# Two transformer layers over 416 edge groups: scores, softmax and sums in three stages, or in one chunked loop

## The chip, the cores and the metric

The kernel runs on one core of one Trainium2 chip. The metric is the time of one execution on the device in microseconds, from a few runs, lower is better. The profile is of one further execution.

## What is computed

A chain of graph layers over 3125 nodes with 128 features and 50000 edges, sorted by destination: a relational layer, a GCN with batch norm, a GATv2 layer with a feed-forward part, and at the end two transformer convolutions. Only the last two are restructured. Each computes, with H = 4 heads of C = 32:

```python
q = (x @ Wq + bq).reshape(N, H, C)
k = (x @ Wk + bk).reshape(N, H, C)
v = (x @ Wv + bv).reshape(N, H, C)
alpha = jnp.einsum('ehc,ehc->eh', q[dst], k[src]) / jnp.sqrt(jnp.float32(C))
amax = jax.ops.segment_max(alpha, dst, num_segments=N)
ealpha = jnp.exp(alpha - amax[dst])
denom = jax.ops.segment_sum(ealpha, dst, num_segments=N)
attn = ealpha / denom[dst]
out = jax.ops.segment_sum(attn[..., None] * v[src], dst, num_segments=N)
return out.reshape(N, H * C) + x @ Ws + bs
```

## The kernel before

The nodes lie in 25 windows of 125. The sorted edges are cut into 416 tiles of 128 edges ("pairs" of an edge tile and the one window that its destinations fall in); `pair_win_i` holds each pair's window, read into registers by `windows`. Four pairs are a group (G = 4), so there are 104 groups. One transformer layer is five blocks, one after the other, with all engines joined between them:

- `conv_nodes` computes q, k, v and the skip term for all nodes and stores k and v to `kv_table` in DRAM.
- `conv_scores`: GpSimd (POOL) issues four indirect gathers a group (L917) that bring the k and v rows of the edges' sources into a ring of eight groups, `got`. SyncE (SP) stores the v half to `v_rows` in DRAM. VectorE (DVE) makes a one-hot of the destinations (L927); TensorE (PE) turns it (L1801), ScalarE (ACT) copies it (L1787), and PE multiplies it with q (L1814), in fp32. Two score banks `q_b` alternate. DVE multiplies with k (L1775), reduces by head (L1778) and scales (L1780).
- `segment_softmax` takes the maximum over each destination's edges for all 416 x 4 columns at once: transposes on PE, scans and element-wise passes on DVE, then one exponential on ACT into `small`.
- `conv_sums` runs over double groups of eight pairs: SP loads the stored v rows, DVE makes the one-hots (L1064) and the messages (L1068), GpSimd splits the weights into three bf16 parts (L998 to L1004). PE adds messages (fp32, L1092) and weights (bf16, 12 columns, L1093) into all eight PSUM banks, at the address of the pair's window, and after every second pair adds a product of 512 zero columns to the last bank (L1097). Before its loop it issues 16 of these as well (L1082).
- `conv_finish` divides, adds the skip term and normalizes at the end.

The loops of PE, DVE, ACT and SP are hardware loops (`Fori`); that of GpSimd in `conv_scores` is written out. Each engine works through its own instructions in order.

## Time and profile before

| | |
|---|---|
| median of 3 runs | 4879.6 us (4878.93 to 4885.05) |
| profiled execution, its time | 4863.76 us |
| span of that execution | 4862.0 us |
| first transformer layer, first gather to last sum read | 3181.6 to 3968.7 us |
| second transformer layer, first gather | 4026.2 us |
| mean granted TensorE clock | 0.716 |

### The profile page before, as it was taken

Reading aid. Unit: us, or ns where it says so; the run is one execution under the profiler, and the core shown is the slowest. Engines: PE = TensorE matmul, PEld = TensorE weight load, DVE = VectorE, ACT = ScalarE, POOL = GpSimd, SP = SyncE. Lnnn points to the kernel's source line nnn. Section 1 sums busy time; section 2 is a strip of 40 time slices with the busy share of each in tenths; the row PEclk is TensorE's granted clock in tenths of the full one; section 3 lists DMA queues with packets and bytes.
Section 4 is the critical chain, followed back from the end, with each engine's and each line's share of the span. In section 5 each row is a group of like instructions: output and inputs, shape, how many; then the busy total and the mean of one; then the engine's idle time right before and its main releaser. Section 6 shows DMA issues by size and latency. Waiting matters only on the chain. (4 is left out here: it accounts for less than half of the span.)

```text
span 4862.0 us, 67990 instructions
## 1 busy us (share of the span) xinstructions
PE 3211.9 (66%) x15577; PEld 2186.9 (45%) x15578; DVE 2813.1 (58%) x9606; ACT 888.8 (18%) x2002; POOL 2734.6 (56%) x3193
## 2 busy tenths in 40 slices
PE   6766677743433259999996998544443984444395
PEld 3235566633333224555543444434443863444284
DVE  8997454431111586676767888744444663444476
ACT  1000111110000021111114777311110211111021
POOL 0016677327777047555535886067774746777373
PEclk9985555555555579999998999855555995555597
DMA  1111122211111104233321221045553435555342
GB/s 61 39 38 45 43 53 53 26 33 51 50 50 50 31 1 103 77 80 79 78 46 43 67 69 49 15 141 153 152 153 93 142 100 143 153 154 154 87 150 83
DMA packets 320800, 387.80 MB, mean 80 GB/s; under 512 B 45989, under 2 KB 230133, under 8 KB 320618
## 3 DMA queue, kind: packets, MB, share of 16 engines
q0 software_dynamic: 80000, 192.10, 15.7%
q1 hardware_dynamic: 240618, 193.80, 13.2%
q14 instruction: 132, 1.08, 0.1%
q8 instruction: 50, 0.82, 0.1%
HBM read 279.89 MB, written 105.84 MB: 79 GB/s over the span
## 5 line engine op out<-in xcount | busy, mean ns | idle before, releaser
L917 POOL DMA_INDIRECT got<-kv_table,pair_src x832 | 814.9, 979 | 497.5 <-issue 252.9
L559 POOL DMA_INDIRECT y_got<-y_table,y_idx x416 | 399.0, 959 | 505.3 <-SPq L511 338.2
L927 DVE TENSOR_TENSOR hot<-pair_dst,iota 128x500 bf16<-128x500 f32 (+1 forms) x424 | 289.3, 683 | 511.0 <-PE sums L990 474.0
L917 POOL DMA_INDIRECT got<-t_table,pair_src x416 | 414.8, 997 | 267.9 <-ACTq L953 141.5
L917 POOL DMA_INDIRECT got<-x_table,pair_src x420 | 398.3, 948 | 286.2 <-issue 283.3
L1801 PE MATMUL hot_b<-ident_b,hot 128*125 128x128 bf16 x840 | 144.1, 327 | 566.5 <-DVE hot L927 566.4
L1439 DVE SCALAR_TENSOR_TENSOR junk<-z,att 128x128 f32<-128x128 f32 x1664 | 381.4, 287 | 179.1 <-PE z L1497 178.1
L1775 DVE TENSOR_TENSOR prod<-q_b,got 128x512 f32<-128x512 f32 x208 | 143.8, 692 | 570.4 <-DMA got<-kv_table,pair_src 538.8
L1493 PE MATMUL z<-gat_wl,got_t 128*128 128x512 f32 x832 | 432.1, 600 | 0.0
L990 PE MATMUL sums<-got,hot 128*125 128x128 f32 x832 | 214.7, 438 | 328.2 <-DMA got<-t_table,pair_src 328.2
L1202 PE MATMUL sums<-msg,hot 128*125 128x512 f32 x832 | 405.3, 636 | 29.2 <-POOL msg L1143 29.2
L1814 PE MATMUL q_b<-acc,hot_t 125*128 x1664 | 420.1, 434 | 0.1
L1801 PEld LDWEIGHTS hot_b<-ident_b,hot 128*125 128x125 bf16 x840 | 105.2, 217 | 628.5 <-DVE hot L927 628.5
L1814 PEld LDWEIGHTS q_b<-acc,hot_t 125*128 125x128 f32 x1664 | 380.1, 333 | 0.5 <-issue 0.5
L990 PEld LDWEIGHTS sums<-got,hot 128*125 128x125 f32 x832 | 184.3, 326 | 359.1 <-issue 359.1
L1497 PE MATMUL z<-xr,hot_t 125*128 x1248 | 336.1, 377 | 0.0
L1188 DVE TENSOR_TENSOR acc<-acc,sums 125x536 f32 x416 | 295.2, 710 | 52.5 <-PE sums L1206 8.3
L1787 ACT CAST hot_t<-hot_b 125x512 f32<-125x512 bf16 x210 | 123.2, 587 | 1010.3 <-PE hot_b L1801 1010.1
L1092 PE MATMUL sums<-msg,hot 128*125 128x128 f32 x1664 | 301.4, 296 | 5.7
L1092 PEld LDWEIGHTS sums<-msg,hot 128*125 128x125 f32 x1664 | 272.0, 188 | 32.5 <-issue 20.3
L1143 POOL TENSOR_TENSOR msg<-rows,wts 128x512 f32<-128x512 f32 x208 | 247.2, 1207 | 36.3 <-DVE wts L1172 33.4
L683 DVE SCALAR_TENSOR_TENSOR hot_w<-iota,src_loc,psum 128x125 f32<-128x125 f32 x416 | 115.2, 339 | 256.9 <-PE psum L795 256.9
(410 smaller groups left out, 6314.8 us busy)
## 6 DMA issues: line engine op xcount, KB each, us to landing
v_rows<-got SPq DMA_DIRECT2D x208, 256.0 KB, 3.2
rows<-v_rows SPq DMA_DIRECT2D x104, 512.0 KB, 3.7
x_rows<-got SPq DMA_DIRECT2D x104, 256.0 KB, 2.6
rows<-x_rows SPq DMA_DIRECT2D x104, 256.0 KB, 2.6
got<-kv_table,pair_src POOLq DMA_INDIRECT x832, 2.9
y_table<-y_stage SPq DMA_DIRECT2D x25, 500.0 KB
got<-x_table,pair_src POOLq DMA_INDIRECT x420
y_got<-y_table,y_idx POOLq DMA_INDIRECT x416, 2.5
```

Source lines behind the costliest of these rows:

```text
L559: pool.indirect_dma_start(out=got[:, slot, j, :], out_offset=None, in_=y_table[:, :], in_offset=bass.IndirectOffsetOnAxis(ap=m.y_idx[:, co ...
L917: pool.indirect_dma_start(out=self.got[:, slot, j, :], out_offset=None, in_=self.table[:, :], in_offset=bass.IndirectOffsetOnAxis(ap=self. ...
L927: v.tensor_tensor(self.hot[:, b, :, :], bc_last(m.pair_dst[:, cols], Q), bc_mid(m.iota[:, 0:Q], G), ALU.is_equal).then_inc(self.hot_ready, 1)
L990: last = t.matmul(sums[0:Q, bass.ds(ws[j] * D, D)], loop.hot[:, b, j, :], loop.got[:, slot, j, :], start=False, stop=False)
L1092: t.matmul(sums[0:Q, bass.ds(ws[j] * D, D)], hot[:, b, j, :], msg[:, b, j, :], start=False, stop=False)
L1188: v.tensor_tensor(row, row, sums[j][0:Q, 0:H * D + 6 * H], ALU.add).then_inc(read, 1)
L1202: t.matmul(sums[j][0:Q, 0:H * D], hot[:, b, j, :], msg[:, b, j, :], start=True, stop=True)
L1439: last = v.scalar_tensor_tensor(junk[:, j, h, :], z[j][:, h * D:(h + 1) * D], 0.0, m.att[:, h * D:(h + 1) * D], ALU.max, ALU.mult, accum_o ...
L1493: t.matmul(z[j][:, :], got_t[:, b, j, :], m.gat_wl[:, :], start=True, stop=False)
L1497: last = t.matmul(z[j][:, :], hot_t[:, b, j, :], m.xr3[:, bass.ds(ws[j], 1), k, :].rearrange("q o d -> q (o d)"), start=False, stop=(k == 2))
L1801: last = t.transpose(hot_b[b][0:Q, j * P:(j + 1) * P], hot[:, b, j, :], m.ident_b[:, :])
L1814: last = t.matmul(q_b[b][:, j * P:(j + 1) * P], hot_t[:, b, j, :], m.acc[:, bass.ds(w, 1), 0:D].rearrange("q o d -> q (o d)"), start=True, ...
```

## The change

`conv_scores`, `segment_softmax` and `conv_sums` of the transformer layers become one block, `conv_layer`, with all loops written out. The pairs are divided into four chunks of 32, 32, 24 and 16 groups. In each chunk, each step scores one group; in the first steps of a chunk (16, 16 and 12 of them) the step also handles two groups of the chunk before (messages on DVE, `add` on PE). At the end of each chunk comes its softmax. The last chunk's 16 groups of sums follow at the end.

Other parts of it: the one-hots for the scores are no longer turned on PE. The destinations are written once as rows to DRAM (`dst_rows`), ACT's queue loads 512 of them broadcast to 125 partitions for each group, and one DVE comparison (`turn_hot`) makes the turned one-hot. Seven PSUM banks hold sums (25 x 128 columns) and weights (25 x 4 columns); the eighth, `work`, is the single bank for scores and softmax. The weights are summed in fp32 with four columns; GpSimd's split, ACT's bf16 copy and the products with zero columns inside the sums are gone. Destinations whose edges cross a chunk's end get an extra row of their own, 125 + chunk (`pair_row`), which is scaled and added back (`rejoin`) at the end; the tables for it are worked out on DVE at the end of `gcn_nodes`. The scale of the scores moves into the weights of q. `alpha` and the scan penalties are laid out by chunk, so in `sort_edges`, `segment_softmax` (still used by the GATv2 layer) and `gat_scores` some operations are cut in four, and the DVE loop of `gat_scores` becomes four loops. The gathers are as before.

```diff
-assert TILES * P >= E and FULL + W <= PAIRS and Q * W == N
+CHUNK = (128, 128, 96, 64)
+CHUNK_AT = tuple(sum(CHUNK[:c]) for c in range(len(CHUNK)))
+assert TILES * P >= E and FULL + W <= PAIRS and Q * W == N and sum(CHUNK) == PAIRS and all(n % 32 == 0 for n in CHUNK)
...
+def chunk_view(flat, c):
+    return flat[:, H * CHUNK_AT[c]:H * (CHUNK_AT[c] + CHUNK[c])].rearrange("l (h p) -> l h p", h=H)
...
+            link(v.tensor_copy(loc[:, :], loc_b[:, 0:3]))
+            link(v.tensor_scalar(m.pair_row[:, :], m.pair_dst[:, 0:PAIRS], float(Q), float(P), ALU.is_ge, ALU.mult))
+            link(v.tensor_tensor(m.pair_row[:, :], m.pair_row[:, :], m.pair_dst[:, 0:PAIRS], ALU.add))
+            for b in range(len(CHUNK) - 1):
+                at, n = CHUNK_AT[b], CHUNK[b]
+                pairs, one = slice(at, at + n), slice(b, b + 1)
+                link(v.tensor_scalar(cont[:, one], m.cont_pen[:, at + n:at + n + 1], -1.0, None, ALU.is_gt))
...
+                link(v.tensor_scalar(mark[:, 0:n], m.pair_win[:, pairs], m.pair_win[:, at + n - 1:at + n], None, ALU.is_equal))
+                link(v.scalar_tensor_tensor(mark[:, 0:n], m.pair_dst[:, pairs], loc[:, one], mark[:, 0:n], ALU.is_equal, ALU.mult))
+                link(v.scalar_tensor_tensor(m.pair_row[:, pairs], mark[:, 0:n], move[:, one], m.pair_row[:, pairs], ALU.mult, ALU.add))
...
+            nc.vector.tensor_scalar(w4[:, 0, :], w4[:, 0, :], float(C) ** -0.5, None, ALU.mult)
+            nc.vector.tensor_scalar(b4[:, 0, :], b4[:, 0, :], float(C) ** -0.5, None, ALU.mult).then_inc(scaled, 1)
+            dve.wait_ge(scaled, 1)
...
-def conv_scores(nc, m, kv_table, v_rows):
...
+def groups_of(c):
+    return range(CHUNK_AT[c] // G, (CHUNK_AT[c] + CHUNK[c]) // G)
+def sums_due(c, k):
+    if not c:
+        return ()
+    before = groups_of(c - 1)
+    return before[2 * k:2 * k + 2]
...
+def conv_layer(nc, m, kv_table, dst_rows, v_rows):
...
+        psum = bank("psum", (P, 8 * 512))
+        dens, work = W * D, psum[:, 7 * 512:8 * 512]
...
+            def load(s):
+                sp.wait_ge(aside[s % 8], 16 * (s // 8 + 1))
+                if s >= 3:
+                    sp.wait_ge(msg_ready, s - 2)
+                sp.dma_start(rows[:, s % 3, :, :], v_rows[s, :, :].rearrange("l (j d) -> l j d", j=G)).then_inc(row_back[s % 3], 16)
+            for c in range(len(CHUNK)):
+                for k, g in enumerate(groups_of(c)):
+                    sp.wait_ge(come[g % 8], 16 * G * (g // 8 + 1))
+                    sp.dma_start(v_rows[g, :, :].rearrange("l (j d) -> l j d", j=G), got[:, g % 8, :, D:2 * D]
+                                 ).then_inc(aside[g % 8], 16)
+                    if c:
+                        due = sums_due(c, k)
+                        ahead = min(due.stop + 2 if len(due) else loaded, groups_of(c - 1).stop)
+                        while loaded < ahead:
+                            load(loaded)
+                            loaded += 1
+            while loaded < groups:
+                load(loaded)
+                loaded += 1
...
+            def turn_hot(g):
+                dve.wait_ge(row_in[g % 3], 16 * (g // 3 + 1))
+                if g >= 2:
+                    dve.wait_ge(q_done, g - 1)
+                v.tensor_scalar(hot_t[:, g % 2], dst_row[:, g % 3, :].rearrange("q (w j l) -> q w j l", w=2, j=2), m.lane[0:Q, :], None,
+                                ALU.is_equal).then_inc(hot_t_ready, 1)
+            def score(c, g):
+                at = g * G - CHUNK_AT[c]
+                dve.wait_ge(q_done, g + 1)
+                dve.wait_ge(come[g % 8], 16 * G * (g // 8 + 1))
+                v.tensor_tensor(prod[:, g % 2, :, :], work.rearrange("p (j d) -> p j d", j=G), got[:, g % 8, :, 0:D], ALU.mult
+                                ).then_inc(used, 1)
+                if g + 1 < groups:
+                    turn_hot(g + 1)
+                dve.wait_ge(used, g + 1)
+                v.reduce_sum(chunk_view(m.alpha, c)[:, :, at:at + G],
+                             prod[:, g % 2, :, :].rearrange("p j (h c) -> p h j c", h=H), AX).then_inc(scored, 1)
+            def messages(s):
+                c = 0
+                while s not in groups_of(c):
+                    c += 1
+                at = s * G - CHUNK_AT[c]
+                w = wts[:, c % 2, 0:H * CHUNK[c]].rearrange("l (h p) -> l h p", h=H)[:, :, at:at + G]
+                if s >= 2:
+                    dve.wait_ge(summed, s - 1)
+                v.tensor_tensor(hot[:, s % 2],
+                                m.pair_row[:, s * G:(s + 1) * G].rearrange("l (w j) -> l w j", w=2).unsqueeze(3).broadcast_to([P, 2, 2, P]),
+                                m.iota[:, 0:P].unsqueeze(1).unsqueeze(1).broadcast_to([P, 2, 2, P]), ALU.is_equal)
+                dve.wait_ge(row_back[s % 3], 16 * (s // 3 + 1))
+                dve.wait_ge(exped, c + 1)
+                v.tensor_tensor(msg[:, s % 2, :, :].rearrange("l j (h c) -> l j h c", h=H),
+                                rows[:, s % 3, :, :].rearrange("l j (h c) -> l j h c", h=H),
+                                w.rearrange("l h j -> l j h").unsqueeze(3).broadcast_to([P, G, H, C]), ALU.mult).then_inc(msg_ready, 1)
...
+            turn_hot(0)
+            for c in range(len(CHUNK)):
+                for k, g in enumerate(groups_of(c)):
+                    score(c, g)
+                    for s in sums_due(c, k):
+                        messages(s)
+                softmax(c)
...
+            for s in groups_of(last_chunk):
+                messages(s)
+            dve.wait_ge(shares_ready, 1)
+            dve.wait_ge(closed, 1)
+            for b in range(last_chunk):
+                w, = windows(nc, m.pair_win_i, ENG.DVE, CHUNK_AT[b + 1] - 1, 1)
...
+            for g in range(groups):
+                if g >= 3:
+                    act.wait_ge(hot_t_ready, g - 2)
+                act.dma_start(dst_row[:, g % 3, :], row_bc(dst_rows[g, :], Q)).then_inc(row_in[g % 3], 16)
+                if done < last_chunk and g == groups_of(done).stop + 2:
+                    act.wait_ge(shifted, done + 1)
+                    nc.scalar.activation(wts[:, done % 2, 0:H * CHUNK[done]], carried[:, 0, 0:H * CHUNK[done]], ACT.Exp).then_inc(exped, 1)
+                    done += 1
...
+            def query(c, k, g):
+                ws = windows(nc, m.pair_win_i, ENG.PE, g * G, G)
+                pe.wait_ge(hot_t_ready, g + 1)
...
+                if g:
+                    pe.wait_ge(used, g)
+                if c and not k:
+                    pe.wait_ge(low_read, c)
                 for j in range(G):
-                    last = t.transpose(hot_b[b][0:Q, j * P:(j + 1) * P], hot[:, b, j, :], m.ident_b[:, :])
+                    last = t.matmul(work[:, j * P:(j + 1) * P], hot_t[:, g % 2, j // 2, j % 2, :],
+                                    m.acc[:, bass.ds(ws[j], 1), 0:D].rearrange("q o d -> q (o d)"), start=True, stop=True)
+                last.then_inc(q_done, 1)
+            def add(c, s):
+                ws = windows(nc, m.pair_win_i, ENG.PE, s * G, G)
+                w = wts[:, c % 2, 0:H * CHUNK[c]].rearrange("l (h p) -> l h p", h=H)
+                pe.wait_ge(msg_ready, s + 1)
+                for j in range(G):
+                    t.matmul(psum[:, bass.ds(ws[j] * D, D)], hot[:, s % 2, j // 2, j % 2, :], msg[:, s % 2, j, :], start=False, stop=False)
+                    last = t.matmul(psum[:, bass.ds(ws[j] * H + dens, H)], hot[:, s % 2, j // 2, j % 2, :],
+                                    w[:, :, s * G + j - CHUNK_AT[c]], start=False, stop=False)
+                last.then_inc(summed, 1)
...
+                t.matmul(work[:, 0:cols], m.only127[:, :], top[:, 0:cols], start=True, stop=True).then_inc(high_ready, 1)
+                pe.wait_ge(high_read, c + 1)
+                t.matmul(work[:, 0:cols], m.only0[:, :], top[:, 0:cols], start=True, stop=True).then_inc(low_ready, 1)
...
+            for k in range(7):
+                t.matmul(psum[:, k * 512:(k + 1) * 512], zeros[:, 0:P], zeros[:, :], start=True, stop=False)
+            for c in range(len(CHUNK)):
+                for k, g in enumerate(groups_of(c)):
+                    query(c, k, g)
+                    for s in sums_due(c, k):
+                        add(c - 1, s)
+                softmax(c)
+            for s in groups_of(last_chunk):
+                add(last_chunk, s)
...
-            conv_scores(nc, m, kv_table, v_rows)
-            segment_softmax(nc, m)
-            conv_sums(nc, m, v_rows)
+            conv_layer(nc, m, kv_table, dst_rows, v_rows)
```

## Rows read from the trace of the kernel before

**Rows 1.** Page: span, and granted clock in 40 slices (tenths).

```profile
span 4862.0 us, 67990 instructions
...
PEclk9985555555555579999998999855555995555597
```

**Rows 2.** Windows: scores, softmax, sums of the first layer (columns: head row).

```profile
core 0: us, PE busy (x) PEld busy (x) DVE busy (x) ACT busy (x) POOL busy (x), PEclk, DMA share, GB/s
3181.00:3722.40 541.40, 260.70 (x1252) 230.00 (x1252) 232.68 (x418) 61.60 (x105) 409.38 (x416) 0.50 0.55 151
3722.40:3775.20 52.80, 14.07 (x42) 8.87 (x42) 30.76 (x15) 4.34 (x2) 0.08 (x1) 0.60 0.01 3
3775.20:3968.70 193.50, 185.95 (x1488) 169.42 (x1488) 134.84 (x159) 53.32 (x52) 144.22 (x209) 0.99 0.45 141
```

**Rows 3.** Groups by line, first transformer layer (busy us, mean ns, idle before).

```profile
L917 POOL DMA_INDIRECT got<-kv_table,pair_src x416 | 409.4, 984 | 304.1 <-POOLq L55 177.7 <-issue 126.4
...
L1775 DVE TENSOR_TENSOR prod<-q_b,got 128x512 f32<-128x512 f32 x104 | 71.9, 691 | 288.0 <-DMA got<-kv_table,pair_src 266.9 <-PE q_b L1814 21.0
...
L1778 DVE TENSOR_REDUCE score<-prod 128x16 f32<-128x512 f32 x104 | 71.3, 686 | 3.5
...
L1068 DVE TENSOR_TENSOR msg<-rows,wts 128x1024 f32<-128x1024 f32 x52 | 66.2, 1274 | 2.2 <-DMA rows<-v_rows 2.2
L1064 DVE TENSOR_TENSOR hot<-pair_dst,iota 128x1000 f32<-128x1000 f32 x52 | 62.4, 1200 | 0.0
```

**Rows 4.** Timeline of one group of scores (start, duration in us, engine, line).

```profile
3400.30 0.94 POOL L917 DMA_INDIRECT got<-kv_table,pair_src  x1 [0.30 <-issue]
...
3401.55 1.16 POOL L917 DMA_INDIRECT got<-kv_table,pair_src  x1 [0.30 <-issue]
...
3402.42 2.02 PE L1814 MATMUL q_b<-acc,hot_t 125*128 x8
...
3404.60 0.69 DVE L1775 TENSOR_TENSOR prod<-q_b,got 128x512 f32<-128x512 f32 x1 [2.71 <-DMA got<-kv_table,pair_src]
```

**Rows 5.** Timeline of TensorE in the sums stage, two pairs.

```profile
3783.06 0.38 PE L1092 MATMUL sums<-msg,hot 128*125 128x128 f32 x2
3783.28 0.17 PE L1093 MATMUL sums<-wts,hot_b 128*125 128x12 bf16 x1
3783.30 0.46 PE L1092 MATMUL sums<-msg,hot 128*125 128x128 f32 x2
...
3783.88 0.38 PE L1092 MATMUL sums<-msg,hot 128*125 128x128 f32 x2
```

**Rows 6.** Timeline: fp32 matmuls of 8 moving columns in the attention stage.

```profile
1701.46 1.77 PE L1316 MATMUL g_lin<-w_lin,xt 128*125 128x8 f32 x15 [0.40 <-ACT xt L257]
```

**Rows 7.** Timeline of VectorE in the softmax stage.

```profile
3730.90 3.62 DVE L155 TENSOR_TENSOR_SCAN carried<-start_turned,sg_low 128x1664 f32<-128x1664 f32 x1 [8.53 <-PE sg_low L122]
...
3756.23 1.89 DVE L172 TENSOR_TENSOR ends<-carried,cont_pen 128x1660 f32<-128x1660 f32 x1
```

**Rows 8.** Windows of other stages: TensorE busy time beside the granted clock.

```profile
600.00:640.00 40.00, 29.67 (x172) 25.68 (x170) 19.66 (x103) 6.82 (x18) 30.25 (x33) 0.50 0.21 53
1756.00:1760.00 4.00, 2.45 (x4) 0.67 (x4) 3.93 (x11) 0.94 (x3) 2.36 (x2) 0.73 0.00 0
1760.00:1764.00 4.00, 3.36 (x4) 1.15 (x4) 3.97 (x10) 1.03 (x2) 2.35 (x2) 0.50 0.00 0
...
3730.00:3732.00 2.00, 0.87 (x5) 0.47 (x3) 1.10 (x1) 0.00 (x0) 0.00 (x0) 0.82 0.00 0
```

**Rows 9.** Timeline of TensorE inside the first of these windows.

```profile
642.53 0.59 PE L788 MATMUL psum<-ident_b,hot_rel 128*24 128x128 bf16 x4 [1.29 <-DVE hot_w L683]
643.05 2.07 PE L809 MATMUL psum<-y_got,hot_w 128*125 128x128 f32 x8
644.91 0.55 PE L814 MATMUL psum<-dw_hot,dl_hot 128*125 128x32 bf16 x4
645.39 0.60 PE L795 MATMUL psum<-inv_t,rel_t 24*128 x4
```

More of the change, by code:

```diff
@@ L832, in make_link, with gcn_nodes @@
     return link
-def gcn_nodes(nc, m, ins, t_table):
+def gcn_nodes(nc, m, ins, t_table, dst_rows):
     with ExitStack() as ctx:
@@ L873, in _ @@
         def _(pe):
+            for k in range(PAIRS // RB):
+                last = nc.tensor.transpose(dst_b[0:RB, k * P:(k + 1) * P], m.pair_dst[:, k * RB:(k + 1) * RB], m.ident[:, :])
+            last.then_inc(dst_turned, 1)
+            for b in range(3):
+                at = CHUNK_AT[b + 1] - 1
+                last = nc.tensor.matmul(loc_b[:, b:b + 1], m.only127[:, :], m.pair_dst[:, at:at + 1], start=True, stop=True)
+            last.then_inc(loc_ready, 1)
             pe.wait_ge(x_ready, 1)
@@ L1714, in _ @@
             pe.wait_ge(copied, TG)
+            pe.wait_ge(scaled, 1)
             pe.wait_ge(loaded, 128)
@@ new lines, in _ @@
+            go(v.tensor_copy(m.h[:, :, :].rearrange("q w d -> q (w d)"), psum[0:Q, 0:W * D]))
+            link(v.tensor_copy(m.dens[:, :, :].rearrange("q w h -> q (w h)"), psum[0:Q, dens:dens + W * H]))
+            for b in range(last_chunk):
+                w, = windows(nc, m.pair_win_i, ENG.DVE, CHUNK_AT[b + 1] - 1, 1)
+                sums, ws = m.h[:, bass.ds(w, 1), :].rearrange("q o d -> q (o d)"), m.dens[:, bass.ds(w, 1), :].rearrange("q o h -> q (o h)")
+                dve.wait_ge(rejoined, 1)
+                go(v.tensor_tensor(sums, sums, work[0:Q, b * (D + H):b * (D + H) + D], ALU.add))
+                link(v.tensor_tensor(ws, ws, work[0:Q, b * (D + H) + D:(b + 1) * (D + H)], ALU.add))
@@ L1819, in conv_finish @@
+            for k in range(7):
+                last = t.matmul(psum[:, k * 512:(k + 1) * 512], zeros[:, 0:P], zeros[:, :], start=False, stop=True)
+            last.then_inc(closed, 1)
+            pe.wait_ge(parts_ready, last_chunk)
+            for b in range(last_chunk):
+                last = t.matmul(work[0:Q, b * (D + H):(b + 1) * (D + H)], m.rejoin[:, b, :], part[:, b, :], start=True, stop=True)
+            last.then_inc(rejoined, 1)
 def conv_finish(nc, m, last_layer, out):
```

371 lines of the change are left out of this document (191 added, 180 removed).

## The prediction

> **What bounds the kernel now.** I read the page first [rows 1]: only the last third of the span, from slice 26 on, holds the restructured layers, and there the granted clock falls to 0.5 in the scores and stands near full in the sums. The windows by stage give one layer: 541.4 us of scores, 52.8 of softmax, 193.5 of sums, together 787.7 us [rows 2]; the second layer has the same shape. The stages have different bounds. In the scores GpSimd is the pace: 416 gathers at 984 ns with 0.30 us between them [rows 3, 4] make 416 x 1.28 = 534 us, and DVE waits 266.9 us for gathers at the product L1775 [rows 3]. All else there is slack: PE is busy 260.7 of 541.4 us, at clock 0.50. In the sums PE is the pace: 185.95 busy of 193.5 us, at clock 0.99 [rows 2]. So the idea of laying the sums under the gathers has up to some 193 + 53 us a layer to win. The question is whether a step with both is shorter than what it replaces, and at which clock PE does it.
>
> **What one pass costs.** Eight fp32 passes of 128 columns take 2.02 us in the scores, with 0.3 us of run-out some 0.21 us each; this is clock 0.50 [rows 4, 2]. In the sums a pair of pairs repeats every 0.82 us (3783.06 to 3783.88): four such passes, two small bf16 products and one of 512 zero columns. Two neighbouring pairs start 0.22 us apart for two fp32 passes [rows 5], so 0.107 us a pass at full clock. The weights' new product has four moving columns in fp32. The nearest row is the one with eight: 15 passes in 1.77 us, 0.10 to 0.12 us each [rows 6]; so little can be saved by few columns, because each pass loads 128 columns of weights again. I take 0.107 us at full clock and, doubled like the others, 0.214 at half. Could the small pass be nearly free? Then a group's sums would cost half; that end is kept for the range.
>
> **One step that only scores.** Chain: product 0.69, `turn_hot` (not in the trace: a one-input comparison of 512 elements, between half of and the whole 0.69 of L1778; I take 0.4), eight passes 1.71, run-out and handovers 0.4: 3.2 us at half clock. The gathers take 5.1 us (4 x 1.28). So these steps stay at the gathers' pace, unless the ring holds groups in advance; then they run at 3.2.
>
> **One step with two groups of sums.** The order of each engine's instructions decides. PE has query(g), add(2k), add(2k+1), query(g+1). DVE has score(g), messages(2k), messages(2k+1), score(g+1). Since `score(g+1)` waits for `query(g+1)`, which stands behind both adds, and the adds wait for messages that stand behind `score(g)`, the two engines take turns:
>
> - DVE alone: product 0.72, `turn_hot` 0.4, reduction 0.72, one-hot 0.7, first message 0.7 (half of L1064's 1200 ns and of L1068's 1274, with start costs [rows 3]) = 3.25 us.
> - PE: two adds of 4 pairs x 4 passes = 32 passes, then 8 of the query: 40 passes = 8.56 us at half clock, 4.28 at full. The second group's messages (1.4 us) lie under the first add.
> - handovers and run-out: 0.4 us.
>
> That makes 12.2 us at half clock, 7.9 at full. There are 16 + 16 + 12 = 44 such steps and 60 that only score. In either case the gathers (5.1 us) run ahead, fill the ring of eight, and GpSimd stands still.
>
> **Which clock?** Stretches with alternation of PE work and pauses: in the relational stage PE is busy 29.67 of 40 us, in bursts of about 3.5 us with pauses of 1.29 us, and the clock stays at 0.50 [rows 8, 9]. In the stage at 1756 to 1764 us it drops from 1.00 and comes back, PE being busy 2.45 of 4 us in the window where it falls and 3.36 in the one at 0.50 [rows 8]. In the softmax it rises for a moment after three microseconds of back-to-back transposes (the last window of [rows 8]). The sums hold full clock, but with a 512-column product of zeros after every second pair and PE busy 185.95 of 193.5 us [rows 2, 5]. The new steps have neither: the zero products are gone, four of eight passes of each pair move only four columns, and after every burst PE pauses 3.6 us. That resembles the two stages with pauses, not the sums. I take half clock for all steps, and for the last 16 groups too.
>
> The Trainium skill (TensorE: Matmul & The Clock Gate, Part 1) says that the half rate is the default and sustained activity releases it. A burst of 8.6 us is sustained by its words, and by them the full-clock case below would hold; the relational stage shows steady work that isn't rewarded, but its bursts are shorter. No row here shows which of the two applies.
>
> **Softmax by chunk.** Scans cost 3.62 / 1664 = 2.2 ns an element, passes 1.89 / 1660 = 1.14 ns [rows 7]. For 512 columns: four scans 4.5 us (two of them cut in four, +0.6), some eight passes 5.0, small operations with their waits 1.5, PE's eight transposes and four passes of 512 columns 3.8, handovers 2.5: about 18 us, during which nothing else is scored. 384 columns about 15, 256 about 11. Together 62 us, against 52.8.
>
> **The sum for one layer.** First chunk at the gathers' pace, 32 x 5.1 = 163, with start and landing (541.4 less 104 x 5.12) 9: 172. Then 18 + 16 x 12.2 (195) + 16 x 3.2 (51; the ring is full, and its refill of eight groups, 41 us, fits) + 18 + 195 + 8 x 3.2 (26) + 15 + 12 x 12.2 (146) + 4 x 3.2 (13) + 11 = 860 us to the end of the last softmax. The tail lies behind everything: exponential and first message 3, then 16 groups x 16 passes x 0.214 = 55. Closing the banks and copying them out 6, rejoining the three cut destinations 8, an estimate from small chained operations of 0.1 to 0.5 us. Total 932 against 787.7, 144 us more; twice: +289 us.
>
> **The rest.** The tables at the end of `gcn_nodes`: 35 chained DVE operations of 0.1 to 0.5 us, 7 us, of which the storing of `t_table` hides some 3: +4. `conv_nodes` waits for the scaled weights: +1. Cut operations in `sort_edges`, `segment_softmax`, `gat_scores`: each short, +0 to +3; `gat_scores` is paced by PE. The rows of destinations (104 loads of 125 x 1 KB a layer) are asked for two steps early, and any row of a gather's 1.28 us is shorter than that: hidden; a late one would cost its step about one gather's time. SP's loads of v rows wait for the first message of a step and return within it; behind them on SP's queue stands the next store of v, needed only eight groups later. Written-out loops: no row prices instruction loading, and I take nothing for it; if it stalled an engine 1 us a step, that is 100 us a layer at most, and below nothing lie only the branches saved. Together +7. Profiled time 4864 + 289 + 7 = 5160; the median lies 16 above the profiled time: 5175 us.
>
> **Rivals.**
> 1. *Full clock in the bursts and after them.* The step is 7.9: 44 x 4.3 = 189 less, tail 27 less: 716 us a layer, 72 less than before. 4880 - 144 + 7 = about 4745 us. This is the case on the other side; with the tail at half clock it decides at a step of 12.2 - 144 / 44 = 8.9 us, and of the known costs only the clock can bring that. For it: bursts of 8.6 us. Against: the pauses. Chance 0.14.
> 2. *The clock swings:* it rises late in each burst and falls in the pause, as at 1756 us. About 1.7 us a step saved: 144 - 75 = 69 a layer more, 5025 us. Chance 0.14.
> 3. *The gathers stay the only bound, the sums vanish under them* (the change does what its form promises): 541 + last softmax 11 + tail 58 + closing 14 = 624 a layer, 164 less, about 4560 us. It needs DVE and PE to overlap within a step, which the order forbids. Chance 0.03.
> 4. *DVE and GpSimd hinder each other.* A gather beside DVE's two-input one-hot took 1.16 us in place of 0.94 [rows 4]. Messages are four such operations a step; if each lost as much, either way, 44 x 0.9 = 40 us a layer more: 5255. Chance 0.09. The Trainium skill (SBUF — State Buffer, on the shared port pair) calls it a lock held for a whole instruction; the row shows a delay of 0.2 us, less than a whole instruction.
> 5. The change costs and gains cancel, so that nothing happens: only by accident, chance 0.02.
>
> My forecast, half clock throughout: 0.58, with its own range 5080 to 5240 (passes of four columns from somewhat cheaper to 0.214 us, softmax 62 +- 12). If the four-column passes were free, 16 x 0.214 = 3.4 us a step and 27 of the tail would go, and this case too would end near 4820.
>
> **Numbers.** Range 4760 to 5250: it leaves out half of rival 1, rival 3 and half of 4, some 15 in 100. Faster by over 0.2% (about what a measurement of this kernel can tell from no change): rivals 1 and 3, and 0.03 of the forecast's chance for nearly free passes, 0.2. Same 0.02. Slower 0.78.
>
> **What the profile after would show.** Granted clock near 0.50 in the windows of the double steps; steps 12 us apart, between first passes of two queries; DVE idle in them, released by PE; the passes of four columns as far apart as those of 128; GpSimd idle in the double steps, released by DVE (ring full), and the pace 5.1 us in the first chunk; four gaps of 18, 18, 15 and 11 us; 3.4 us a group in the tail. A clock of 1.00 in these windows, or steps below 9 us, makes the prediction wrong.

## The result, and the profile after

| | before | after |
|---|---|---|
| median | 4879.27 us (4877.56 to 4885.05, 4 runs) | 5154.19 us (5145.73 to 5157.44, 4 runs) |
| profiled execution, its time | 4863.76 us | 5145.73 us |
| span of that execution | 4862.0 us | 5144.0 us |

The ratio is 1.0559, interval 1.0540 to 1.0577: slower, as forecast. The page of the kernel after (granted clock in 40 slices, and the costliest groups of the new block over both layers):

```profile
PEclk9985555555555789999989997555555565555555
...
L1754 POOL DMA_INDIRECT got<-kv_table,pair_src x832 | 834.3, 1003 | 1095.9 <-DVE h L1808 483.5
L1949 PE MATMUL psum<-h,acc 128*128 128x128 f32 x1664 | 645.6, 492 | 304.3 <-DVE h L1829 304.3
L1808 DVE TENSOR_TENSOR h<-psum,got 128x512 f32<-128x512 f32 x208 | 143.8, 691 | 995.2 <-PE psum L1940 780.0
...
L1949 PEld LDWEIGHTS psum<-h,acc 128*128 128x128 f32 x1664 | 450.4, 331 | 331.2 <-issue 331.2
...
L1950 PEld LDWEIGHTS psum<-wts,acc 128*128 128x128 f32 x1664 | 454.6, 333 | 0.0
...
L1950 PE MATMUL psum<-wts,acc 128*128 128x4 f32 x1664 | 355.6, 284 | 0.0
```

Read it against [rows 1, 3]. From the 26th of the 40 slices on, which begins at 3215 us, just behind the layer's first gather, the clock is at 0.5 nearly throughout; the two stretches near full clock that the sums had are gone. The product that ends a group's scoring (L1775 before, L1808 now) was released by gathers; now 780.0 of its 995.2 us of waiting are for `query`'s passes (L1940). And the other way round PE waits 304.3 us for DVE's messages (L1829): each waits for the other. GpSimd waits 483.5 us for DVE to free a place in the ring. The narrow passes (L1950) load as many weights as the wide ones (L1949): 454.6 and 450.4 us of weight loads.

A double step is one that scores a group and adds up two; a single step only scores; the tail is the last chunk's 16 groups of sums. Windows of the first layer after (first chunk, the second chunk's double steps, the length of one double step, 20 us of the tail):

```profile
core 0: us, PE busy (x) PEld busy (x) DVE busy (x) ACT busy (x) POOL busy (x), PEclk, DMA share, GB/s
3196.60:3365.00 168.40, 70.12 (x266) 58.47 (x265) 54.50 (x97) 1.28 (x1) 127.84 (x134) 0.50 0.68 180
3383.00:3571.00 188.00, 139.63 (x629) 135.29 (x630) 64.94 (x112) 0.00 (x0) 79.73 (x77) 0.50 0.45 138
3441.00:3453.00 12.00, 8.94 (x42) 8.65 (x42) 4.08 (x7) 0.00 (x0) 4.33 (x4) 0.50 0.39 120
4060.00:4080.00 20.00, 20.00 (x96) 20.00 (x95) 7.28 (x13) 0.00 (x0) 0.00 (x0) 0.50 0.29 79
```

In a double step PE works 8.94 us and DVE 4.08 of 12, and only about one microsecond of it at the same time. The timeline of VectorE in one of these steps shows DVE's side:

```profile
3442.20 0.69 DVE L1808 TENSOR_TENSOR h<-psum,got 128x512 f32<-128x512 f32 x1 [7.87 <-PE psum L1940]
3442.81 0.48 DVE L1801 TENSOR_SCALAR acc<-dst_row,lane 125x512 f32<-125x512 bf16 x1
3443.20 0.68 DVE L1813 TENSOR_REDUCE alpha<-h 128x16 f32<-128x512 f32 x1
3443.80 0.68 DVE L1824 TENSOR_TENSOR acc<-pair_row,iota 128x512 f32<-128x512 f32 x1
3444.40 0.68 DVE L1829 TENSOR_TENSOR h<-small,wts 128x512 f32<-128x512 f32 x1
3445.00 0.69 DVE L1824 TENSOR_TENSOR acc<-pair_row,iota 128x512 f32<-128x512 f32 x1
3445.60 0.69 DVE L1829 TENSOR_TENSOR h<-small,wts 128x512 f32<-128x512 f32 x1
3454.16 0.69 DVE L1808 TENSOR_TENSOR h<-psum,got 128x512 f32<-128x512 f32 x1 [7.87 <-PE psum L1940]
```

and that of TensorE in the same step the other:

```profile
3445.22 0.79 PE L1949 MATMUL psum<-h,acc 128*128 128x128 f32 x2 [3.06 <-DVE h L1829]
3445.80 0.43 PE L1950 MATMUL psum<-wts,acc 128*128 128x4 f32 x2
3446.09 0.77 PE L1949 MATMUL psum<-h,acc 128*128 128x128 f32 x2
...
3451.78 0.43 PE L1950 MATMUL psum<-wts,acc 128*128 128x4 f32 x2
3452.06 2.06 PE L1940 MATMUL psum<-acc 125*128 x8
```

Follow one turn. At 3442.20 DVE multiplies; at 3445.08 its first message is ready; at 3445.22 PE begins 32 passes of sums; at 3452.06, without a gap, follow the eight of the query; at 3454.12 they are out, and at 3454.16 DVE multiplies again, 11.96 us after the last time. DVE had been idle since its second message at 3446.29, PE for 3.06 us before its first pass. Four passes, two wide and two narrow, take 0.85 us (3445.22 to 3446.09 is 0.87, the next rows 0.85): 0.214 each, of either width.

### The profile page after: what moved, and what is told of

Same layout as the page of the kernel before. It is cut to its first block and busy times, and to the rows that moved or that the text cites. A ratio compares the mean times of both kernels' runs of the same rounds, so it can differ in the third digit from the quotient of the medians.

```text
span 5144.0 us, 62934 instructions
## 1 busy us (share of the span) xinstructions
PE 3486.9 (68%) x15135; PEld 2472.8 (48%) x15140; DVE 2727.0 (53%) x9731; ACT 658.4 (13%) x1697; POOL 2474.1 (48%) x2775
## 5 line engine op out<-in xcount | busy, mean ns | idle before, releaser
L1754 POOL DMA_INDIRECT got<-kv_table,pair_src x832 | 834.3, 1003 | 1095.9 <-DVE h L1808 483.5
L1949 PE MATMUL psum<-h,acc 128*128 128x128 f32 x1664 | 645.6, 492 | 304.3 <-DVE h L1829 304.3
L1808 DVE TENSOR_TENSOR h<-psum,got 128x512 f32<-128x512 f32 x208 | 143.8, 691 | 995.2 <-PE psum L1940 780.0
L1949 PEld LDWEIGHTS psum<-h,acc 128*128 128x128 f32 x1664 | 450.4, 331 | 331.2 <-issue 331.2
L1940 PE MATMUL psum<-acc 125*128 x1664 | 429.3, 440 | 264.0 <-DVE acc L1801 254.3
L969 POOL DMA_INDIRECT got<-t_table,pair_src x416 | 425.4, 1023 | 271.5 <-ACTq L1005 145.0
L1940 PEld LDWEIGHTS psum<-acc 125*128 125x128 f32 x1664 | 374.4, 330 | 306.8 <-issue 306.8
L1950 PEld LDWEIGHTS psum<-wts,acc 128*128 128x128 f32 x1664 | 454.6, 333 | 0.0
L979 DVE TENSOR_TENSOR hot<-pair_dst,iota 128x500 f32<-128x500 f32 (+1 forms) x212 | 145.1, 685 | 489.9 <-PE sums L1042 484.7
L1950 PE MATMUL psum<-wts,acc 128*128 128x4 f32 x1664 | 355.6, 284 | 0.0
L1117 ACT ACTIVATE msg<-rows,wts 128x128 f32<-128x128 f32 x832 | 254.1, 387 | 1.4 <-DMA rows<-x_rows 1.4
```

The lines of the kernel that those rows point to most:

```text
L969: pool.indirect_dma_start(out=self.got[:, slot, j, :], out_offset=None, in_=self.table[:, :], in_offset=bass.IndirectOffsetOnAxis(ap=self. ...
L1754: pool.indirect_dma_start(out=got[:, slot, j, :], out_offset=None, in_=kv_table[:, :], in_offset=bass.IndirectOffsetOnAxis(ap=m.pair_src[: ...
L1940: last = t.matmul(work[:, j * P:(j + 1) * P], hot_t[:, g % 2, j // 2, j % 2, :], m.acc[:, bass.ds(ws[j], 1), 0:D].rearrange("q o d -> q (o ...
L1949: t.matmul(psum[:, bass.ds(ws[j] * D, D)], hot[:, s % 2, j // 2, j % 2, :], msg[:, s % 2, j, :], start=False, stop=False)
L1950: last = t.matmul(psum[:, bass.ds(ws[j] * H + dens, H)], hot[:, s % 2, j // 2, j % 2, :], w[:, :, s * G + j - CHUNK_AT[c]], start=False, s ...
```

## The experiments

Two theories stand against each other throughout. The first: a double step is 12 us because the order of PE's instructions makes the two engines take turns, and because PE is granted half its clock. The rivals: the gathers or GpSimd bound it after all; or PE's clock alone does it, and turns are only a symptom; or PE's work by itself, narrow passes included, is the bound.

All runs but `e5_no_weights` and `e7_zeros_only` ran on two chips where the kernel before takes 5381 to 5385 us, not 4863; so each is compared with the kernel before on the same chip, and `after_again` is the changed kernel on such a chip.

### after_again: the changed kernel beside the others

No edit.

> The changed kernel, unaltered, as the measure for the runs beside it: in the four runs before this one gathers landed up to 20 us late now and then, so that their totals (the kernel before took 5382 us there) say little of the steps. With prompt gathers: 1.056 times the kernel before. Where gathers land late, less of a difference is expected, since the changed kernel's longer steps hide them.

5676.64 us against 5381.07: 1.0557 (1.0536 to 1.0577), the ratio of the first comparison, where a smaller difference was expected. The time between DVE's products (L1808) tells what such a chip does differently. In the first layer the 44 double steps take 526.2 us in all, as in the first profile of this kernel. But the first chunk's 31 steps take 215.6 in place of 157.6, and the 25 later single steps 133.1 in place of 85.0. The differences lie in the shorter steps, and late gathers are what the expectations put them down to. The rows speak against that. Here is the start of the layer in `e2_order` (below): three products in the timeline of VectorE; a row each of those of SyncE and TensorE; and the view of DVE's waits for gathers (L1807) up to 3544 us:

```profile
3534.30 0.69 DVE L1808 TENSOR_TENSOR h<-psum,got 128x512 f32<-128x512 f32 x1 [3.23 <-DMA got<-kv_table,pair_src]
3543.09 0.69 DVE L1808 TENSOR_TENSOR h<-psum,got 128x512 f32<-128x512 f32 x1 [7.11 <-DMA dst_rows<-dst_t]
3564.80 0.69 DVE L1808 TENSOR_TENSOR h<-psum,got 128x512 f32<-128x512 f32 x1 [20.04 <-DMA dst_rows<-dst_t]
...
3543.67 0.51 SPq L1773 DMA_DIRECT2D v_rows<-got  x1
3544.31 2.07 PE L1940 MATMUL psum<-acc 125*128 x8 [6.72 <-DVE h L1808]
...
L1807 DVEq EVENT_SEMAPHORE  x4: 21/21/21, 3529.3 to 3543.8; - x4
```

Two steps of the chunk are over 20 us long. The product of 3564.80 belongs to the layer's fourth group, whose query is the row of 3544.31. By the code it waits for two things: the group's four gathers and the last pass of its query. The gathers had landed: SyncE, which waits for the same count of the same semaphore, stored this group's v rows at 3543.67, and DVE itself passed its wait for them at 3543.8. The query's passes are recorded as done at 3546.38, and still the product starts 18.4 us after that. The releaser named, a store of `dst_rows` at 1213 us, is an earlier user of the semaphore that the query's last pass raises. So what comes late is PE's word to DVE that the query is done, not the gathers; why, no run shows. In the first layer of `after_again` 24 products of 104 start late by this measure (over 0.3 us behind the query's last pass, SyncE's store and DVE's own work), 155 us in all; in the runs on the chips of 4863 us there is one, of 0.4 us. The other runs on the chips of 5381 us have 138 to 177 us of it a layer, about two thirds of that in the first chunk, so that their totals can be set beside each other to some 20 us a layer.

### e2_order: the query ahead of the sums

```diff
             for c in range(len(CHUNK)):
+                query(c, 0, groups_of(c)[0])
                 for k, g in enumerate(groups_of(c)):
-                    query(c, k, g)
+                    if g + 1 in groups_of(c):
+                        query(c, k + 1, g + 1)
                     for s in sums_due(c, k):
                         add(c - 1, s)
```

The same passes, in another order: `query(g+1)` waits only for DVE's product of `g`, and DVE's messages lie under it.

> The changed kernel with TensorE's order alone altered: query(g+1) is issued before the two adds of step g, so that VectorE's work and the adds can lie side by side. Theory A (half the loss is the turn-taking): at clock 0.50 a step falls from 12.0 to TensorE's own 40 passes, 8.6 to 8.9 us; 44 steps x 3.2 = 140 us less a layer, about 4870 us, near the kernel before. If the denser work brings the full clock, a step is 5.5 to 6 us and the gathers pace the loop: about 4600 us. Rival (VectorE and GpSimd block each other, or loads come late): the step stays above 10 us, over 5000 us.

5380.17 us, 1.0003 (0.9990 to 1.0017) of the kernel before. Run twice more:

> TensorE's order alone altered, once more. The steps were 8.6 us at clock 0.50 in the first run. With prompt gathers: 44 x 3.4 us less a layer, twice 150 us below the changed kernel: some 4850 to 4870 us, 0.995 times the kernel before. Rival (the totals of the first runs were right and the order is worth nothing): as slow as the changed kernel.

> The same kernel as e2_order, once more: the query moved ahead of the sums, no zero products. On a chip where the kernel before takes about 4870 us, a step with sums is 40 passes of 0.214 us = 8.56 us if gathers are never late, so 44 x 3.4 = 150 us a layer less than after (5154 us): about 4855 us, ratio 0.995 to 1.0. Rival (the order is worth more or less where gathers are in time): outside 0.985 to 1.01.

5371.51 us, 0.9983 (0.9970 to 0.9996), and 5376.47 us, 0.9984 (0.9971 to 0.9997). Against `after_again` the order alone takes 296 to 305 us off, some 150 a layer, with no pass fewer. A window of the second chunk, and products of VectorE there:

```profile
3800.00:3820.00 20.00, 20.00 (x96) 20.00 (x95) 10.09 (x17) 0.00 (x0) 8.23 (x9) 0.50 0.64 180
```

```profile
3819.66 0.69 DVE L1808 TENSOR_TENSOR h<-psum,got 128x512 f32<-128x512 f32 x1 [0.62 <-PE psum L1940]
3828.20 0.69 DVE L1808 TENSOR_TENSOR h<-psum,got 128x512 f32<-128x512 f32 x1 [0.62 <-PE psum L1940]
```

A step is 8.53 us, which is 40 passes of 0.213; PE has no pause left. Turn-taking is shown to cost 3.4 us a step (11.96 less 8.53), and PE's own work at half clock is the next bound. The clock stays at 0.50 though PE is busy 20.00 of 20 us: the pauses alone were not what held it down. The third run's expectation is for a chip where the kernel before takes 4870 us; it ran on one of 5385.

### e1_clock: full clock, the order left as it is

```diff
                 for k, g in enumerate(groups_of(c)):
                     query(c, k, g)
+                    if sums_due(c, k):
+                        for _ in range(14):
+                            t.matmul(psum[:, 0:512], zeros[:, 0:P], zeros[:, :], start=False, stop=False)
                     for s in sums_due(c, k):
                         add(c - 1, s)
...
                 for j in range(G):
+                    if j % 2:
+                        t.matmul(psum[:, 0:512], zeros[:, 0:P], zeros[:, :], start=False, stop=False)
                     t.matmul(psum[:, bass.ds(ws[j] * D, D)], hot[:, s % 2, j // 2, j % 2, :], msg[:, s % 2, j, :], start=False, stop=False)
```

The zero products fill PE's pause; the turns stay.

> The changed kernel with products of 512 zero columns added (nothing they add changes a result): one after every second pair of a group's sums, and 14 in each step with sums, between its query and its first add, where TensorE pauses. Theory A, the clock at 0.50 makes the steps 12 us long: the fill brings TensorE to full clock, a step takes about 8.8 us (pause 3.25, 32 passes and 4 zero products 4.3, query 0.86, handovers 0.4), the tail 34 us; some 160 us less a layer, 4830 us in all. Theory B, the turn-taking and not the clock: were the clock to stay at 0.50, the 14 products take 6.0 us, more than the pause, and the four more 1.7: steps of 16 us, 5500 us. In between: a clock that swings, 5000 to 5200.

5382.1 us, 1.0008 (0.9994 to 1.0021). A window of 20 us in the double steps of the second chunk, and TensorE's timeline:

```profile
3793.00:3813.00 20.00, 19.76 (x134) 14.49 (x137) 10.49 (x19) 0.00 (x0) 9.13 (x9) 1.00 0.52 159
```

```profile
3792.90 1.14 PE L1940 MATMUL psum<-acc 125*128 x8
3794.09 2.97 PE L1980 MATMUL psum<-zeros 128*128 128x512 bf16 x13
3797.10 0.48 PE L1951 MATMUL psum<-h,acc 128*128 128x128 f32 x2
...
3801.20 1.03 PE L1940 MATMUL psum<-acc 125*128 x7
```

At clock 1.00 the step is 8.30 us: query 1.19, filling 3.01 (13 of its 14 products are in the record), sums 4.10. So the clock, less what the four zero products among the sums cost, is worth 3.66 us a step and 294 us in all against `after_again`, as much as the order alone. 88 x 3.66 would be 322; part of the rest is the tail, where this edit doesn't raise the clock and its own zero products make the time from the last product of one layer to the first of the next 155.4 us in place of 148.7. The two are separate costs of about one size, and neither alone puts the change over 0.2% ahead of the kernel before.

### e3_order_zeros: the order, and a zero product for every second pair

The edit of `e2_order` with that of `e1_clock` inside `add` (not the 14).

> The order of the run before, and one product of 512 zero columns after every second pair of the sums, as the kernel before has. Theory A: TensorE has 32 passes, 8 of the query and 4 zero products a step; at full clock 5.1 us, so that the gathers' 5.0 to 5.5 us set the pace and a layer takes about 104 x 5.1 + softmax at the end 11 + tail 35 + 17 = 595 to 640 us: 4510 to 4600 us. If the clock stays at 0.50: 8.6 + 1.7 = 10.3 us a step, about 5000 us.

> Order and one zero product for every second pair, once more. The clock swung between 0.57 and 1.00 in the first run, steps of 5.0 to 9.6 us. With prompt gathers: about half of the steps at full clock, 44 x 5 us less a layer: some 4700 us, 0.96 times the kernel before. If prompt gathers let TensorE keep the full clock: 4540 us, 0.93.

5287.79 us, 0.9833 (0.9782 to 0.9884), and 5265.15 us, 0.9801 (0.9773 to 0.9830). The clock doesn't hold; neither case of the expectations came about. Windows in the double steps, and one of the tail of the same kernel:

```profile
3780.00:3800.00 20.00, 18.85 (x164) 18.40 (x166) 12.52 (x22) 0.00 (x0) 13.56 (x12) 1.00 0.79 223
3800.00:3820.00 20.00, 16.29 (x88) 15.97 (x88) 11.37 (x19) 0.00 (x0) 11.85 (x12) 0.66 0.67 195
...
4310.00:4330.00 20.00, 19.76 (x94) 19.10 (x94) 6.46 (x10) 0.00 (x0) 0.00 (x0) 0.50 0.16 39
```

At full clock the double steps are short, the one-hots of the messages start late after PE's passes, as the products do in `after_again` (70 us in all in the first layer), PE pauses, the clock falls, and the next steps are long again. In the tail, with no pause, this mix of passes stays at 0.50.

### e6_order_zeros2: the order, and a zero product for every pair

The edit of `e2_order`, and inside `add` the zero product without the condition `j % 2`.

> As the run before, but one product of 512 zero columns for every pair, eight a step. Theory A (the clock is held by what lies between the narrow passes): full clock in all steps with sums and in the tail; a step is 4.28 + 8 x 0.213 = 6.0 us, the tail 41 us, a layer 646 us in place of 787.7: 4600 us, 0.945 times the kernel before. Rival: the clock swings with the pauses in the steps that only score, whatever is put into the sums; then as the run before or slower, 4700 us or more.

> The same kernel as e6_order_zeros2, once more. Its first run stood beside a kernel before of 5381 us, where gathers landed late, and gave 0.9686 in place of the 0.945 expected. Theory (late gathers took the rest): where the kernel before takes about 4870 us the ratio is 0.94 to 0.955, about 4630 us; where it takes 5381 us again, 0.967 to 0.971. Rival (turn-taking is not all gone, or the zero products cost more than they give): 0.968 on either chip.

5210.29 us, 0.9686 (0.9665 to 0.9707), and 5214.15 us, 0.9685 (0.9670 to 0.9700): the fastest of the versions that do all the work, 3% ahead of the kernel before. Twice as many zero products as in `e3_order_zeros`, and faster. Windows of the second chunk and of the tail:

```profile
3780.00:3800.00 20.00, 19.04 (x160) 18.14 (x159) 11.34 (x19) 0.00 (x0) 13.49 (x12) 0.98 0.76 224
3800.00:3820.00 20.00, 17.81 (x145) 16.84 (x145) 12.66 (x22) 0.00 (x0) 11.91 (x12) 0.96 0.75 221
...
4280.00:4300.00 20.00, 20.00 (x176) 19.03 (x175) 11.64 (x18) 0.00 (x0) 0.00 (x0) 1.00 0.32 93
```

and VectorE's products:

```profile
3784.34 0.68 DVE L1808 TENSOR_TENSOR h<-psum,got 128x512 f32<-128x512 f32 x1
3789.93 0.69 DVE L1808 TENSOR_TENSOR h<-psum,got 128x512 f32<-128x512 f32 x1
3799.74 0.69 DVE L1808 TENSOR_TENSOR h<-psum,got 128x512 f32<-128x512 f32 x1 [1.61 <-DMA dst_rows<-dst_t]
3803.83 0.68 DVE L1808 TENSOR_TENSOR h<-psum,got 128x512 f32<-128x512 f32 x1
```

An undisturbed step is 5.59 us, close to the gathers' 5.1; 12 of the 44 are 9 to 11.4 us. The 44 double steps of the layer take 294 us where 44 x 5.59 would be 246, and the first chunk is 57 us above what it takes on the chip of 4863 us. The expectation of 0.945 was missed. The second run's case for the chip of 5381 us (0.967 to 0.971) came true, but that it would be 0.94 to 0.955 on one of 4870 us could not be tried: its kernel before took 5384.98 us. Late gathers, the reason given in that expectation, are not what the trace shows. The product of 3799.74 has its query recorded as done at 3795.26, and SyncE stored its gathered v rows at 3793.74. In these 44 steps products start 8 us in all, and the one-hots of the messages (L1824) 60 us in all, later than PE's last pass that they wait for and DVE's own work; GpSimd is not behind, for it stands idle 100 us beyond its usual 0.30 between gathers. So late word from PE is large enough for the missing 48 us, and it stays open what this version is worth elsewhere.

### e7_zeros_only: a zero product for every pair, the old order

```diff
                 for j in range(G):
+                    t.matmul(psum[:, 0:512], zeros[:, 0:P], zeros[:, :], start=False, stop=False)
                     t.matmul(psum[:, bass.ds(ws[j] * D, D)], hot[:, s % 2, j // 2, j % 2, :], msg[:, s % 2, j, :], start=False, stop=False)
```

> The changed kernel's order, with one product of 512 zero columns for every pair of the sums, eight a step, and nothing in TensorE's pause. If full clock comes back in spite of the pauses: step 3.25 + 0.4 + 4.28 + 1.7 = 9.6 us less what lies under the messages, about 9.3; 0.995 to 1.01 times the kernel before. If the pause of 3.6 us takes it away each time: at 0.50 the step is 12.0 + 8 x 0.427 = 15.4 us, 1.11 times. A swing gives 1.03 to 1.08.

4949.69 us against 4862.47 on that chip: 1.0179 (1.0149 to 1.0208). That lies between the cases expected (up to 1.01 with the clock held, from 1.03 with a swing). Most steps take 10.24 to 10.36 us, all 44 of the first layer 455, and this is the clock inside one of them, in windows of 1 us:

```profile
3440.00:3441.00 1.00, 0.00 (x0) 0.00 (x0) 1.00 (x3) 0.00 (x0) 0.21 (x1) 1.00 0.00 0
3441.00:3442.00 1.00, 0.00 (x0) 0.00 (x0) 1.00 (x2) 0.00 (x0) 0.74 (x1) 1.00 0.04 12
3442.00:3443.00 1.00, 0.23 (x1) 0.24 (x2) 1.00 (x3) 0.00 (x0) 0.96 (x1) 0.79 0.58 137
3443.00:3444.00 1.00, 1.00 (x6) 0.97 (x6) 0.92 (x2) 0.00 (x0) 0.69 (x2) 0.50 0.66 144
...
3446.00:3447.00 1.00, 1.00 (x9) 0.94 (x10) 0.00 (x0) 0.00 (x0) 0.03 (x1) 1.00 1.10 357
```

PE pauses at full clock, the clock falls at the end of the pause, the first part of the burst runs at 0.50 and the rest at 1.00. This is rival 2 of the prediction, brought about by this edit: 1.6 to 1.7 us a step less than 11.96. That this is about the rival's price of 1.7 is partly luck, since eight zero products a step, which the rival doesn't have, are in it. Here the clock falls with each pause. On this chip, turn-taking keeps the change behind the kernel before even with a better clock.

### e5_no_weights: without the narrow passes

```diff
                 for j in range(G):
-                    t.matmul(psum[:, bass.ds(ws[j] * D, D)], hot[:, s % 2, j // 2, j % 2, :], msg[:, s % 2, j, :], start=False, stop=False)
-                    last = t.matmul(psum[:, bass.ds(ws[j] * H + dens, H)], hot[:, s % 2, j // 2, j % 2, :],
-                                    w[:, :, s * G + j - CHUNK_AT[c]], start=False, stop=False)
+                    last = t.matmul(psum[:, bass.ds(ws[j] * D, D)], hot[:, s % 2, j // 2, j % 2, :], msg[:, s % 2, j, :], start=False, stop=False)
```

This kernel leaves the sums of the weights out and divides by 1.

> The changed kernel without the sums of the weights: the products of four moving columns are left out, and the last step divides by one instead. Theory A (a narrow fp32 pass costs as much as a wide one): 16 passes less in each step with sums, 12.0 - 3.4 = 8.5 us, and 27 us less in the tail; 178 us a layer, twice, so 1.056 times the kernel before becomes 0.985 to 0.99. Rival (the four-column passes are nearly free): unchanged, 1.05. If full clock returns once all passes are wide, steps are about 6 us and it ends below 0.96.

4716.64 us against 4862.47: 0.9699 (0.9671 to 0.9727), lower than the 0.985 to 0.99 expected. The 44 double steps of the first layer take 352 us, 8.0 each, where 24 passes of 0.214 and the pause at half clock would be 8.5; the tail is 30 us shorter. What was missed is the clock. The window of 20 us in the double steps:

```profile
3421.00:3441.00 20.00, 11.94 (x61) 11.01 (x60) 10.11 (x18) 0.00 (x0) 12.18 (x12) 0.75 0.64 203
```

Without the narrow passes the clock rises to 1.00 at the end of a burst and falls in the pause or early in the next burst (0.75 is the mean of this window, 0.68 of the next); with them it stayed at 0.50. Two steps of three take 7.5 to 7.9 us; every third, where the clock rises only after the burst has ended (last pass at 3423.69, mean clock 0.92 from 3424 to 3425), takes 8.54, the half-clock sum. So leaving them out saves their passes, and some of the clock besides. The bursts are shorter in this run as well; which of the two lets the clock rise was not separated.

### e4_before_nozeros: the kernel before without its zero products

```diff
-            for _ in range(16):
-                t.matmul(sums[0:Q, 7 * 512:8 * 512], zeros[:, 0:Q], zeros[:, :], start=False, stop=False)
             with pe.Fori(0, steps) as i:
...
-                        if j % 2 == 1:
-                            t.matmul(sums[0:Q, 7 * 512:8 * 512], zeros[:, 0:Q], zeros[:, :], start=False, stop=False)
```

> The kernel before without its products of 512 zero columns in the sums (after every second pair, and 16 ahead of the loop). If they hold the clock up there: the sums run at 0.50, 416 pairs x (2 x 0.214 + 0.214) = 270 us a layer in place of 193, 5030 us in all. If the clock doesn't depend on them: 416 x 0.08 = 33 us less a layer, about 4815 us.

5540.65 us against 5381.72: 1.0303 (1.0277 to 1.0329), 159 us more for work taken away. A window of its sums stage, to be set beside the third of [rows 2]:

```profile
4200.00:4240.00 40.00, 40.00 (x191) 40.00 (x191) 19.01 (x24) 8.20 (x8) 21.36 (x32) 0.50 0.36 112
```

PE is busy 40.00 of 40 us at 0.50, where with the zero products it stood at 0.99; the stage takes 263 us in place of 193. So the zero products were worth 80 us a layer to the kernel before. That dropping them is part of the change's loss is what `e1_clock` bears out: with zero products back, its steps run at 1.00.

## Why the prediction was right, point by point

The forecast was half clock throughout, 5175 us; measured 5154.19. In the profiled executions the difference is 282.0 us where 296 was worked out. It lies so: 15.0 ahead of the first gather (3181.6 to 3196.6), 131.7 between the first gathers of the two layers (844.6 to 976.3), and 135.3 after that. The rest of the miss is the step from the profiled time to the median: 16 us assumed, 8.5 this time.

The first layer by the terms of the sum, from the starts of L1808 and the rows around them:

| term | predicted us | measured us |
|---|---|---|
| first chunk | 172 | 167.2 |
| four softmaxes | 18, 18, 15, 11 | 18.5, 19.1, 16.0, 11.9 |
| 44 double steps | 12.2 each, 536 | 11.96 each, 526.2 |
| later single steps | 90 | 89.7 |
| exponential and first message | 3 | 3.0 |
| tail, 16 groups of sums | 55 | 54.8 |
| closing | 14 | 11.3 |
| layer | 932 | 917.7 |

- **The pass.** 0.214 us at half clock for 128 and for 4 columns, as taken. In the 20 us window of the tail PE is busy 20.00 us. At full clock it is 0.11 (four in 0.44 us in `e1_clock`), as taken, though the prediction misread a row for it: two neighbouring pairs start 0.24 us apart in [rows 5] (3783.06 and 3783.30), not 0.22. The end kept for the range, nearly free narrow passes, is excluded by the timeline of the step.
- **The turns.** The order of events is the one written down, and `e2_order` shows that it is a cause: another order, some 150 us a layer less. Of the step's parts, DVE's chain was 2.88 us for 3.25 predicted, because most operations start 0.60 us after the one ahead and not 0.72. Handovers and run-out were 0.5 together for 0.4.
- **The clock.** 0.50 in every double step and in the tail. The reason given, pauses as in the relational stage, was only half of it, so that the right clock came partly by luck. (The timeline of [rows 9] lies just behind its window, from 642.53 on; the clock is 0.50 there too.) `e2_order` has no pause and stays at 0.50; `e4_before_nozeros` likewise. `e7_zeros_only` has zero products and the pause, `e1_clock` zero products and a filled pause, and only the second holds the clock. So two things kept it down. With the change's own mix of passes it never rose, while it did with one zero product per pair, and with the narrow passes left out; one for every second pair was enough in `e1_clock`'s double steps, and not in its tail or in that of `e3_order_zeros`. And where it rose, the pauses of the turns took it away again. Rival 1 (4745 us) expected it from the long bursts; they ran at 0.50. The step at full clock that it counted with, 7.9 us, measured 8.30 in `e1_clock`, with four zero products among the sums at some 0.14 us each.
- By the Trainium skill (TensorE: Matmul & The Clock Gate, Part 1) sustained activity releases the throttle. This case's traces don't bear that out for an engine that the records call busy: 20.00 of 20 us at 0.50 in the tail. The measurement decides.
- **Single steps and gathers.** The first chunk is paced at 5.1 us a step (157.6 / 31), the later single steps take 3.3 to 3.6 us from a full ring, 3.2 predicted.
- **DVE against GpSimd.** A gather beside DVE's two-input operations took 1.49 us in place of 0.95 (start 3444.41 and 3446.20 in GpSimd's timeline of the step), more than the 1.16 of [rows 4]. It cost nothing, since GpSimd then waits 6.72 us for a place in the ring. Rival 4 had its mechanism and no price. The Trainium skill (SBUF — State Buffer, on the shared port pair) has one engine wait for the whole instruction of the other; the delay of 0.54 us stays below one DVE operation's 0.68 and doesn't decide it.
- **The rest.** The term said +7 and the profile shows +15.0 ahead of the first gather, but not where it was put. The first gather of the GCN stage starts at 1049.26 before and 1049.47 after, so that the tables and cut operations cancel with other shifts. Then 416 gathers of unchanged code take 10.6 us longer in all (mean 1023 ns for 997). In `e5_no_weights` and `e7_zeros_only`, with that stage the same as in the changed kernel, first to last gather take 542 and 536 us where the changed kernel took 551 and the one before 540: this stage varies by about as much between executions, so that the 10.6 us can't be laid to the change. In `e7_zeros_only` the first transformer gather comes at 3182.8, only 1.2 us later than before. The last 4.2 us arise between the GCN stage's last gather and the first transformer gather; 1.6 of them in `conv_nodes`, whose first matmuls wait 2.98 us for the scaled bias (1.35 for a load before).

What wasn't separated: the second layer lost 4 us more than the first, and it wasn't followed where. Nor did a run take the written-out loops back; the step's parts leave no room for a stall by them, as they sum to its length.

## What to carry to other kernels

When work of two stages is put into one loop, write down each engine's instructions in order and ask, for each wait, what stands between it and its releaser: here one call placed behind the sums instead of ahead of them cost some 150 us a layer, about as much as the whole change lost. Ask at which clock PE did the work before, and what held it there: zero products that look like waste were worth 159 us to the kernel before. And when an idle engine is the reason to merge two stages, add up the passes first: 40 passes at half clock are 8.5 us beside 5.1 of gathers, so that the merged step is PE's, not the gathers'.

## What the hardware showed that was not expected

- TensorE recorded busy 40.00 of 40 us and granted half its clock (`e4_before_nozeros`), for a whole stage. The changed kernel's passes with one 512-column zero product per pair ran at 1.00 in the tail of `e6_order_zeros2`, with one for every second pair at 0.50 in that of `e3_order_zeros`; for the kernel before, whose narrow products are bf16, one for every second pair was enough for 0.99.
- The clock didn't fall at once when PE stopped. In `e7_zeros_only` it is still 1.00 through whole microseconds of idle time and is 0.50 when the next burst is under way: the burst pays, not the pause. In `e5_no_weights` it even rises in a pause, after a last pass at 3423.69 (mean 0.92 from 3424 to 3425, PE busy 0.00).
- A narrow fp32 pass is no cheaper than a wide one: two of each take 0.85 us at 0.50, and 0.44 at 1.00 (3790.86 to 3791.30 in `e1_clock`). A product of 512 zero columns beside them adds only 0.14 us there (3790.28 to 3790.86 for the same four passes and the product).
- On two chips the kernel before took 5381 to 5385 us, on others 4862 to 4879 (ratios of the changed kernel 1.0557 and 1.0559). On the first two, DVE started up to 19.4 us after TensorE's last pass that it waited for was recorded as done, with the gathers landed; the kernel before shows it too (unchanged scoring loop, first to last product: 621.7 us in `e4_before_nozeros`, 532.2 in the profile before). The double steps of the changed kernel had the same length to 0.1 us on both kinds of chip. Why PE's word comes late is open.
